# Segment attention in one decoder kernel: output projection as three f32r terms at half height, moved values kept once, and three pieces of work reordered

## The chip, the cores and the metric

The kernel runs on one core of one Trainium2 chip. The metric is the device time of one execution in microseconds (us). The engines are TensorE (PE; its weight loads are listed as PEld), VectorE (DVE), ScalarE (ACT), GpSimd (POOL) and SyncE (SP), which here issues every DMA. Each engine works through its own instructions in program order and waits on semaphores that the others raise.

## The reference

Three layers follow one another, each added to its input and layer-normalised: segment attention, cross attention, and a block with full softmax attention. Only the first is touched:

```
x: 4 x 1024 x 256; 16 heads of 64; segments of 128 tokens
q, k, v = x Wq, x Wk, x Wv          per segment reshaped to (head, 128 positions, 64)
gate = sigmoid(betas)
for each segment of a sequence, with mem and z carried along:
    sq   = elu(q) + 1
    mem += sq^T v ;  z += sum(elu(k) + 1)
    dot  = softmax(q k^T / 8) v
    att  = gate * (sq mem / (rowsum(sq) * z)) + (1 - gate) * dot
    out  = att (128 x 1024) @ Wo (1024 x 256)
x = layernorm(x + out)
```

## The kernel before

`emit_segment_attention` makes 16 iterations of 256 tokens, that is of two segments t = 0, 1. One iteration's work is cut into four units u (two per segment, half of the head groups each). Every engine's program is written out by hand as the same two functions called in turn: `preparation(it)` and `attention(it)`. So the order is fixed in the source, and what differs from one version to another is which semaphore comes late.

`attention(it)` (PE from L373) finishes the attention of iteration it and projects the next one, n = it + 1: K (`project_k`), V (`project_v`), Q (`project_q`), each as a sum of three f32r products hi*hi, hi*lo, lo*hi through `split_matmuls` (L38), with turns of the softmax probabilities (`turn_probs`) and the two products of a unit (`attend`: NUM from the memory, PV from the values) in between. At its end PE turns the input of iteration it + 2 (`turn_x`, into X_BANK), which ACT rounds (`high_x`, L446) and DVE subtracts (`low_x`, L637).

`preparation(it)` (PE from L409) computes scores for the four units (`scores`, L284), turns phi(q) (`turn_phi`, L300), forms the memory products (`memory`, L314) and turns the scaled phi (`turn_phin`, L325). The output projection of the iteration before (`project_out`, L368) is laid between these in three pieces of 8, 4 and 4 chunks. DVE at the same time takes the row maxima (`maxima`, L691), makes phi (`make_phi`, L656), copies turned phi (`take_phi`, L700), adds the memory (`add_memory`, L720) and the residual (`residual`, L743). ACT computes the exponentials (`exp_phi`, `exp_scores`), POOL relu(q) and the scaling of probabilities and phi.

The output projection is plain f32: `att` holds gate and keep parts combined (`combine`, L731, on DVE), its rows split over the two halves e of the 128 partitions, so each chunk is two matmuls of 64 rows, one in each half of the array, into two banks (Y_BANK).

Values travel through memory: ACT copies a unit's V out of X_BANK into `v_stage` (`stage_v`, L455), SP stores it (`values_out`, L185), and after all stores have landed loads it in another layout, 32 small DMAs, into `v_pos` (`values_in`, L193). `v_pos` has two copies, by the parity of the iteration, and `v_stage` has room for all four units. SP's order in an iteration is: store of the normalised rows, residual load, input load, the value stores, the value loads. Banks and rings shared between steps are guarded by waits such as the one of `turn_phin` on `y_added` (L318 to L323: the bank is Y_BANK), or of `project_v` on `v_staged` (X_BANK has one unit at a time).

## Time and profile before

| | us |
|---|---|
| median of 3 runs | 1963.51 (1960.6 to 1967.28) |
| the profiled execution's own time | 1964.41 |
| its span, first to last instruction | 1962.6 |
| busy over the span: PE, DVE, ACT, POOL | 1811.5, 1472.6, 1525.0, 548.0 |
| one iteration of segment attention (key projection to key projection, 295.05 to 344.29) | 49.24 |

The span is what the profiler's records cover; the execution's own time is 1.8 us longer. Segment attention takes about 820 us of the span, the other layers the rest. Below, "the frame" means one iteration in the middle, with its trace times: `attention` from 295.05 to 325.88 on PE, `preparation` from 325.88 to 344.29. A record's duration includes a latency of its own, so neighbours on an engine overlap: what one more instruction costs is the distance from start to start, and what a waiter sees is the end.

### The profile page before, as it was taken

Reading aid. Unit: us, or ns where it says so; the run is one execution under the profiler, and the core shown is the slowest. Engines: PE = TensorE matmul, PEld = TensorE weight load, DVE = VectorE, ACT = ScalarE, POOL = GpSimd, SP = SyncE. Lnnn points to the kernel's source line nnn. Section 1 sums busy time; section 2 is a strip of 40 time slices with the busy share of each in tenths; the row PEclk is TensorE's granted clock in tenths of the full one; section 3 lists DMA queues with packets and bytes.
Section 4 is the critical chain, followed back from the end, with each engine's and each line's share of the span. In section 5 each row is a group of like instructions: output and inputs, shape, how many; then the busy total and the mean of one; then the engine's idle time right before and its main releaser. Section 6 shows DMA issues by size and latency. Waiting matters only on the chain. (4 is left out here: it accounts for less than half of the span.)

```text
span 1962.6 us, 45176 instructions
## 1 busy us (share of the span) xinstructions
PE 1811.5 (92%) x16278; PEld 1231.5 (63%) x16378; DVE 1472.6 (75%) x2829; ACT 1525.0 (78%) x4376; POOL 548.0 (28%) x658
## 2 busy tenths in 40 slices
PE   6999999999999999599999989899999899899996
PEld 5888888888888888469999978422222222222264
DVE  7677777777777777246666656799999999999845
ACT  6777777777777777248888856799999999999853
POOL 2343333333333334205676520000000000000023
PEclk9999999999999999899999989899999999999998
DMA  7223333233322332251101009335325334423001
GB/s 172 44 61 60 60 60 61 61 60 60 61 61 60 61 61 55 64 136 32 43 15 43 15 17 224 130 52 77 46 44 74 58 44 58 74 44 44 1 22 64
DMA packets 139653, 121.73 MB, mean 62 GB/s; under 512 B 78747, under 2 KB 111407, under 8 KB 139439
## 3 DMA queue, kind: packets, MB, share of 16 engines
q1 hardware_dynamic: 139439, 118.88, 30.7%
q8 instruction: 134, 2.20, 0.5%
q14 instruction: 80, 0.66, 0.1%
HBM read 77.29 MB, written 41.53 MB: 61 GB/s over the span
## 5 line engine op out<-in xcount | busy, mean ns | idle before, releaser
L1889 DVE TENSOR_REDUCE s_neg_max<-s_ring 128x1 f32<-128x1024 f32 x512 | 588.7, 1215 | 22.7 <-PE s_ring L1804 22.6
L1852 ACT ACTIVATE s_prob<-s_ring,s_neg_max 128x1024 f32<-128x1024 f32 x512 | 570.6, 1115 | 16.6 <-DVE s_neg_max L1889 16.2
L1817 PE MATMUL s_acc<-s_prob,s_v_norm 128*32 128x256 f32 x4096 | 327.7, 393 | 11.6 <-ACT f_zT_all L1844 10.4
L1804 PE MATMUL s_ring<-f_stack 128*128 128x512 bf16 x924 | 292.2, 390 | 33.2 <-issue 14.3
L492 ACT ACTIVATE a_prob<-a_psum,a_neg_max 128x128 f32<-128x128 f32 x512 | 179.8, 377 | 60.6 <-DVE a_neg_max L691 60.6
L1817 PEld LDWEIGHTS s_acc<-s_prob,s_v_norm 128*32 128x32 f32 x4096 | 81.5, 108 | 229.7 <-issue 215.0
L1804 PEld LDWEIGHTS s_ring<-f_stack 128*128 128x128 bf16 x1024 | 58.7, 97 | 244.4 <-ACT s_prob L1852 225.0
L1872 POOL TENSOR_TENSOR s_v_norm<-f_v_all,s_row_inv 128x64 f32<-128x64 f32 x128 | 37.4, 292 | 570.3 <-DVE s_row_inv L1882 570.3
L586 POOL TENSOR_SCALAR a_relu_ring<-a_qT 128x512 f32<-128x512 f32 x64 | 98.6, 1557 | 343.0 <-ACT a_qT L463 315.7
L731 DVE SCALAR_TENSOR_TENSOR a_att<-a_psum,a_keep_cols,a_num_s 128x128 f32<-128x128 f32 x256 | 72.1, 345 | 134.2 <-ACT a_num_s L514 127.5
L1271 ACT ACTIVATE x_prob<-x_psum,x_neg_max 128x77 f32<-128x77 f32 x512 | 160.8, 337 | 14.2 <-DVE x_neg_max L1428 14.1
L38 PE MATMUL a_psum<-a_xT_hi,a_w_hi 128*128 128x256 f32 x512 | 152.9, 299 | 5.8 <-DVE a_w_lo L629 5.8
L38 PE MATMUL a_psum<-a_xT_lo,a_w_hi 128*128 128x256 f32 x512 | 145.2, 284 | 0.0
L38 PE MATMUL a_psum<-a_xT_hi,a_w_lo 128*128 128x256 f32 x512 | 145.2, 284 | 0.0
L602 POOL TENSOR_TENSOR a_prob<-a_prob,a_row_inv 128x512 f32<-128x512 f32 x128 | 137.4, 1099 | 1.6 <-DVE a_row_inv L696 1.6
L1354 POOL TENSOR_TENSOR x_prob<-x_prob,x_row_inv 128x308 f32<-128x308 f32 x128 | 91.7, 717 | 134.0 <-DVE x_row_inv L1434 134.0
L368 PE MATMUL a_psum<-a_w_out,a_att 64*128 64x256 f32 x1024 | 119.9, 379 | 3.9 <-DVE a_att L731 3.8
L647 DVE TENSOR_SCALAR a_kT<-a_psum 64x256 f32<-64x256 f32 x256 | 107.9, 421 | 12.1 <-PE a_psum L38 6.7
L504 ACT COPY a_probT<-a_psum 128x512 f32<-128x512 f32 x128 | 75.5, 590 | 51.4 <-PE a_psum L337 50.7
L492 ACT ACTIVATION_READ_ACCUMULATOR a_prob<-a_psum,a_neg_max 128x1 f32 x512 | 110.6, 216 | 0.0
L1271 ACT ACTIVATION_READ_ACCUMULATOR x_prob<-x_psum,x_neg_max 128x1 f32 x512 | 110.4, 216 | 0.0
L463 ACT COPY a_qT<-a_psum 64x256 f32<-64x256 f32 x256 | 94.0, 367 | 18.1 <-PE a_psum L38 15.5
(199 smaller groups left out, 4101.2 us busy)
## 6 DMA issues: line engine op xcount, KB each, us to landing
f_stack<-qk_thirds SPq DMA_DIRECT2D x256, 128.0 KB, 6.0
segment_values<-a_v_stage SPq DMA_DIRECT2D x64, 256.0 KB, 3.6
a_v_pos<-segment_values SPq DMA_DIRECT2D x512, 32.0 KB
qk_thirds<-p_third SPq DMA_DIRECT2D x16, 768.0 KB, 7.8
a_x_in<-in_x_dram SPq DMA_DIRECT2D x16, 256.0 KB, 3.2
a_x_res<-in_x_dram SPq DMA_DIRECT2D x32, 128.0 KB, 2.8
after_attention<-a_normed SPq DMA_DIRECT2D x32, 128.0 KB, 2.4
x_x_in<-after_attention SPq DMA_DIRECT2D x32, 128.0 KB, 2.1
```

Of the source, the lines that this page charges most:

```text
L38: last = pe.matmul(out, a, b, start=n == 0, stop=n == len(terms) - 1)
L368: last = pe.matmul(Y_BANK[e][:, 0:D], att[rows(e), c, :, :].rearrange("p m i -> p (m i)"), w_out[rows(e), c, :], start=c == 0, stop=c == H ...
L463: last = act.copy(shift_target(qT, r, e, f), shift_source(bank[f], r, e))
L492: last = act.activation(prob[:, u, n, :], bank[2 * (u % 2) + e][:, gi * P:(gi + 1) * P], ACT.Exp, bias=neg_max[:, u, n:n + 1], accum_out=r ...
L586: pool.tensor_scalar(relu_ring[:, u % 2, :], qT[:, m:m + 4, :, :].rearrange("p a b c -> p (a b c)"), 0.0, None, ALU.max).then_inc(q_relu, 1)
L602: pool.tensor_tensor(part, part, row_inv[:, u, 4 * half:4 * half + 4].unsqueeze(2).to_broadcast([P, 4, P]), ALU.mult).then_inc(prob_ready, 1)
L647: last = dve.tensor_scalar(shift_target(kT, r, e, f), shift_source(bank[f], r, e), 1.0 / KEY_DIV, None, ALU.add)
L1271: last = act.activation(prob[:, t % 2, at:at + CTX], S_BANK[g][:, j * CTX:(j + 1) * CTX], ACT.Exp, bias=neg_max[:, t % 2, g, j:j + 1], acc ...
L1804: last = pe.matmul(ring[n % 3][:, f * HALF:(f + 1) * HALF], k_stack[:, slot, j, kt * P:(kt + 1) * P], q_stack[:, slot, j, f * HALF:(f + 1) ...
L1817: last = pe.matmul(acc[32 * j:32 * j + 32, s], v_norm[:, step // KT % 2, step % 4, j, :], prob[:, step % 4, j, s], start=step % (2 * KT) = ...
L1852: act.activation(prob[:, step % 4, j, :], ring[n % 3][:, :], ACT.Exp, bias=neg_max[:, step % 2, j:j + 1], accum_out=row_sum[:, step % 2, j ...
L1889: dve.tensor_reduce(neg_max[:, step % 2, j:j + 1], ring[n % 3][:, :], AX_X, ALU.max, negate=True).then_inc(max_ready, 1)
```

## The change

Four things are changed, all in segment attention.

1. The output projection is a sum of three f32r products. Wo is loaded to a staging place and split into `w_out_hi` and `w_out_lo` once (ACT and POOL, at the start). `combine` now writes its result in place in `num_s`; a new ACT step `high_att` rounds it to `att_hi`, and a new DVE step `low_att` subtracts to give `att_lo`. `project_out` issues per chunk three terms of two half-height matmuls (96 an iteration instead of 32).
2. `v_pos` has one copy, so `values_in` waits for `pv_done` of the iteration before. `v_stage` holds two units instead of four: `stage_v` of units 2 and 3 waits until the stores of units 0 and 1 of the same iteration have landed. The stores are issued per unit, 8 of half the size instead of 4.
3. The input turn moves behind the last `attend` on PE; `high_x` and `low_x` move from `attention` into `preparation`.
4. The scores of unit 3 move on PE from before the last piece of the output projection to between `memory(1)` and `memory(2)`, and on DVE `maxima(it, 3)` moves behind `add_memory` 0 and 1.

On PE, at the end of `preparation` in the middle of the program (a_e_ring is phi before its turn, a_phi_tok phi turned, a_kT and a_qT the operands of the scores). Before:

```order
L284 MATMUL a_psum<-a_kT,a_qT 128x128 [waits a_exp_done]
L284 MATMUL a_psum<-a_kT,a_qT 128x128 x7
L368 MATMUL a_psum<-a_w_out,a_att 128x256 x8
L314 MATMUL a_psum<-a_v_pos,a_phi_tok 64x64 [waits a_v_landed0,a_phi_tok_ready]
L314 MATMUL a_psum<-a_v_pos,a_phi_tok 64x64 x7
L314 MATMUL a_psum<-a_v_pos,a_phi_tok 64x64 [waits a_phi_tok_ready]
L314 MATMUL a_psum<-a_v_pos,a_phi_tok 64x64 x7
L314 MATMUL a_psum<-a_v_pos,a_phi_tok 64x64 [waits a_mem_added,a_v_landed1,a_phi_tok_ready]
L314 MATMUL a_psum<-a_v_pos,a_phi_tok 64x64 x7
L314 MATMUL a_psum<-a_v_pos,a_phi_tok 64x64 [waits a_mem_added,a_phi_tok_ready]
L314 MATMUL a_psum<-a_v_pos,a_phi_tok 64x64 x7
L325 MATMUL a_psum<-a_ident,a_phin 128x128 [waits a_y_added,a_phin_ready]
```

After (L316 was L300, L300 was L284, L386 was L368, L330 was L314, L341 was L325):

```order
L386 MATMUL a_psum<-a_w_out_hi,a_att_lo 128x256 x2
L330 MATMUL a_psum<-a_v_pos,a_phi_tok 64x64 [waits a_v_landed0,a_phi_tok_ready]
L330 MATMUL a_psum<-a_v_pos,a_phi_tok 64x64 x7
L330 MATMUL a_psum<-a_v_pos,a_phi_tok 64x64 [waits a_phi_tok_ready]
L330 MATMUL a_psum<-a_v_pos,a_phi_tok 64x64 x7
L300 MATMUL a_psum<-a_kT,a_qT 128x128 [waits a_exp_done]
L300 MATMUL a_psum<-a_kT,a_qT 128x128 x7
L330 MATMUL a_psum<-a_v_pos,a_phi_tok 64x64 [waits a_mem_added,a_v_landed1,a_phi_tok_ready]
L330 MATMUL a_psum<-a_v_pos,a_phi_tok 64x64 x7
L330 MATMUL a_psum<-a_v_pos,a_phi_tok 64x64 [waits a_mem_added,a_phi_tok_ready]
L330 MATMUL a_psum<-a_v_pos,a_phi_tok 64x64 x7
L341 MATMUL a_psum<-a_ident,a_phin 128x128 [waits a_y_added,a_phin_ready]
```

The scores of unit 3 now stand behind two memory products; the wait of the turn of phin on `a_y_added` is unchanged.

On DVE, from the end of `attention` to the second `maxima` (a_xT_lo is the input's low part, a_neg_max the row maxima). Before:

```order
L684 TENSOR_TENSOR a_z_gate<-a_z_inv,a_gate_cols 128x16 [waits a_z_step]
L637 TENSOR_TENSOR a_xT_lo<-a_psum,a_xT_hi 128x2x2x64 [waits a_xT_hi_ready]
L637 TENSOR_TENSOR a_xT_lo<-a_psum,a_xT_hi 128x2x2x64
L731 SCALAR_TENSOR_TENSOR a_att<-a_psum,a_keep_cols,a_num_s 128x16x8 [waits a_num_scaled,a_pv_done]
L731 SCALAR_TENSOR_TENSOR a_att<-a_psum,a_keep_cols,a_num_s 128x16x8 x3
L691 TENSOR_REDUCE a_neg_max<-a_psum 128x8 [waits a_scores_done]
L656 SCALAR_TENSOR_TENSOR a_e_ring<-a_e_ring,a_relu_ring 128x512 [waits a_q_relu,a_phi_exp] x2
L691 TENSOR_REDUCE a_neg_max<-a_psum 128x8 [waits a_scores_done]
L696 RECIPROCAL a_row_inv<-a_row_sum 128x8 [waits a_exp_done]
```

After (L788 is `low_att`, L780 `combine`, L740 `maxima`, L686 `low_x`):

```order
L788 TENSOR_TENSOR a_att_lo<-a_num_s,a_att_hi 128x4x16x8 [waits a_att_high]
L780 SCALAR_TENSOR_TENSOR a_num_s<-a_psum,a_keep_cols,a_num_s 128x128 [waits a_num_scaled,a_pv_done]
L780 SCALAR_TENSOR_TENSOR a_num_s<-a_psum,a_keep_cols,a_num_s 128x128 x3
L788 TENSOR_TENSOR a_att_lo<-a_num_s,a_att_hi 128x4x16x8 [waits a_att_high]
L740 TENSOR_REDUCE a_neg_max<-a_psum 128x8 [waits a_scores_done]
L686 TENSOR_TENSOR a_xT_lo<-a_psum,a_xT_hi 128x2x2x64 [waits a_xT_hi_ready]
L686 TENSOR_TENSOR a_xT_lo<-a_psum,a_xT_hi 128x2x2x64
L705 SCALAR_TENSOR_TENSOR a_e_ring<-a_e_ring,a_relu_ring 128x512 [waits a_q_relu,a_phi_exp] x2
L740 TENSOR_REDUCE a_neg_max<-a_psum 128x8 [waits a_scores_done]
L745 RECIPROCAL a_row_inv<-a_row_sum 128x8 [waits a_exp_done]
```

`low_x` has moved from ahead of the last `combine` to behind the first `maxima`, and one of the four `low_att` stands ahead of that `maxima`, with a wait on ACT.

On SP, one iteration up to the first value loads. Before:

```order
L179 DMA after_attention<-a_normed 64x2x256 [waits a_normed_ready]
L179 DMA after_attention<-a_normed 64x2x256
L174 DMA a_x_res<-in_x_dram 64x2x256 [waits a_y_added]
L174 DMA a_x_res<-in_x_dram 64x2x256
L164 DMA a_x_in<-in_x_dram 128x2x256 [waits a_x_turned]
L185 DMA segment_values<-a_v_stage 64x1024 [waits a_v_staged]
L185 DMA segment_values<-a_v_stage 64x1024
L185 DMA segment_values<-a_v_stage 64x1024 [waits a_v_staged]
L185 DMA segment_values<-a_v_stage 64x1024
L193 DMA a_v_pos<-segment_values 8x16x64 [waits a_v_stored1,a_v_stored0]
```

After:

```order
L178 DMA a_x_res<-in_x_dram 64x2x256 [waits a_y_added]
L178 DMA a_x_res<-in_x_dram 64x2x256
L168 DMA a_x_in<-in_x_dram 128x2x256 [waits a_x_turned]
L190 DMA segment_values<-a_v_stage 64x512 [waits a_v_staged]
L190 DMA segment_values<-a_v_stage 64x512
L190 DMA segment_values<-a_v_stage 64x512 [waits a_v_staged]
L190 DMA segment_values<-a_v_stage 64x512
L190 DMA segment_values<-a_v_stage 64x512 [waits a_v_staged]
L190 DMA segment_values<-a_v_stage 64x512
L190 DMA segment_values<-a_v_stage 64x512 [waits a_v_staged]
L190 DMA segment_values<-a_v_stage 64x512
L201 DMA a_v_pos<-segment_values 8x16x64 [waits a_pv_done,a_v_stored1,a_v_stored0]
```

The four stores of two waits are eight stores of four waits; what stands ahead of them is the same.

The diff, cut to its core:

```diff
-        v_stage = sb("v_stage", [P, 2, INNER])
-        v_pos = sb("v_pos", [P, 2, 2, H, DH])
+        v_stage = sb("v_stage", [P, 2, HALF])
+        v_pos = sb("v_pos", [P, 2, H, DH])
...
-        stage = [probs[:, 0:2048], probs[:, 2048:4096], att[:, :, :, :].rearrange("p a b c -> p (a b c)")]
+        stage = [probs[:, 0:2048], probs[:, 2048:4096], v_pos[:, :, :, :].rearrange("p a b c -> p (a b c)")]
+        out_stage = [phi_tok[:, :, :].rearrange("p a b -> p (a b)"), probs[:, 0:2048]]
...
-            def values_out(it, e):
-                sp.wait_ge(v_staged, 4 * it + 2 * e + 2)
+            def values_out(it, u):
+                e, half = u // 2, u % 2
+                sp.wait_ge(v_staged, 4 * it + u + 1)
                 for t in range(2):
                     at = it * TOK + t * P + e * DH
-                    sp.dma_start(v_rows[at:at + DH, :], v_stage[rows(t), e, :]).then_inc(v_stored[e], 16)
+                    sp.dma_start(v_rows[at:at + DH, half * HALF:(half + 1) * HALF], v_stage[rows(t), u % 2, :]
+                                 ).then_inc(v_stored[u % 2], 16)
 
             def values_in(it, t):
                 if t == 0:
-                    for e in range(2):
-                        sp.wait_ge(v_stored[e], 32 * (it + 1))
+                    for n in range(2):
+                        sp.wait_ge(v_stored[n], 64 * (it + 1))
+                if it > 0:
+                    sp.wait_ge(pv_done, 4 * (it - 1) + 2 * t + 2)
                 at = it * TOK + t * P
                 for c in range(H):
-                    sp.dma_start(v_pos[c * 8:(c + 1) * 8, it % 2, t, :, :],
+                    sp.dma_start(v_pos[c * 8:(c + 1) * 8, t, :, :],
                                  v_rows[at:at + P, c * DH:(c + 1) * DH].rearrange("(h i) d -> i h d", i=8)
                                  ).then_inc(v_landed[t], 16)
+
+            def load_out(n):
+                if n == 1:
+                    sp.wait_ge(w_low, 1)
+                for e in range(2):
+                    sp.dma_start(out_stage[n][rows(e), :].rearrange("p (c n) -> p c n", n=D),
+                                 wo.rearrange("(c v) n -> v c n", v=DH)[:, n * 8:(n + 1) * 8, :]
+                                 ).then_inc(wo_landed[n], 16)
...
@@ -362,11 +378,14 @@
                 if chunks[0] == 0:
                     pe.wait_ge(att_ready, 4 * it + 4)
                     if it == 0:
-                        pe.wait_ge(wo_landed, 32)
+                        pe.wait_ge(wo_low, 2)
+                terms = ((att_hi, w_out_hi), (att_hi, w_out_lo), (att_lo, w_out_hi))
                 for c in chunks:
-                    for e in range(2):
-                        last = pe.matmul(Y_BANK[e][:, 0:D], att[rows(e), c, :, :].rearrange("p m i -> p (m i)"), w_out[rows(e), c, :],
-                                         start=c == 0, stop=c == H - 1, skip_group_check=True)
+                    for n, (left, right) in enumerate(terms):
+                        for e in range(2):
+                            last = pe.matmul(Y_BANK[e][:, 0:D], left[rows(e), c, :, :].rearrange("p m i -> p (m i)"),
+                                             right[rows(e), c, :], start=c == 0 and n == 0,
+                                             stop=c == H - 1 and n == 2, skip_group_check=True)
...
+                    if old:
+                        attend(it, u)
                     if u == 3 and it + 2 < ITER:
                         turn_x(it + 2)
-                    if old:
...
-                scores(it, 3)
                 if it > 0:
                     project_out(it - 1, range(12, H))
-                for u in range(UNITS):
-                    memory(it, u)
+                memory(it, 0)
+                memory(it, 1)
+                scores(it, 3)
+                memory(it, 2)
+                memory(it, 3)
...
             def stage_v(it, u):
-                e, half = u // 2, u % 2
                 act.wait_ge(v_done, 4 * it + u + 1)
-                if it > 0:
-                    act.wait_ge(v_stored[e], 32 * it)
-                act.copy(v_stage[:, e, half * HALF:(half + 1) * HALF], X_BANK[:, :]).then_inc(v_staged, 1)
+                if it > 0 or u >= 2:
+                    act.wait_ge(v_stored[u % 2], 64 * it + 32 * (u // 2))
+                act.copy(v_stage[:, u % 2, :], X_BANK[:, :]).then_inc(v_staged, 1)
+
+            def high_out(n):
+                act.wait_ge(wo_landed[n], 32)
+                act.copy(w_out_hi[:, 8 * n:8 * n + 8, :].rearrange("p c n -> p (c n)"), out_stage[n]
+                         ).then_inc(wo_high, 1)
+
+            def high_att(it, u):
+                m = (u // 2) * GR + (u % 2) * 4
+                act.wait_ge(combined, 4 * it + u + 1)
+                if u == 0 and it > 0:
+                    act.wait_ge(y_done, it)
+                act.copy(att_hi[:, :, m:m + 4, :].rearrange("p c m i -> p m c i"),
+                         num_s[:, u % 2, :, :].rearrange("p m (c i) -> p m c i", i=8)).then_inc(att_high, 1)
...
@@ -487,6 +520,8 @@
                 act.wait_ge(max_ready, 4 * it + u + 1)
                 if it > 0:
                     act.wait_ge(prob_turned, 8 * (it - 1) + 2 * u + 2)
+                elif u == 0:
+                    act.wait_ge(wo_low, 2)
...
+                if not old:
+                    high_out(0)
...
+                        if u > 0:
+                            high_att(it, u - 1)
...
-                    if u == 3 and it + 2 < ITER:
-                        high_x(it + 2)
+                    if not old and u == 1:
+                        high_out(1)
...
+                if it > 0:
+                    high_att(it - 1, 3)
...
+                if it + 1 < ITER:
+                    high_x(it + 1)
...
+            for n in range(2):
+                pool.wait_ge(wo_high, n + 1)
+                pool.tensor_tensor(w_out_lo[:, 8 * n:8 * n + 8, :].rearrange("p c n -> p (c n)"), out_stage[n],
+                                   w_out_hi[:, 8 * n:8 * n + 8, :].rearrange("p c n -> p (c n)").bitcast(F32),
+                                   ALU.subtract).then_inc(wo_low, 1)
...
                 dve.wait_ge(phi_turned, 4 * it + u + 1)
+                if it == 0 and u == 0:
+                    dve.wait_ge(wo_low, 1)
...
             def combine(it, u):
-                t, half = u // 2, u % 2
+                half = u % 2
                 dve.wait_ge(pv_done, 4 * it + u + 1)
                 dve.wait_ge(num_scaled, 4 * it + u + 1)
-                if u == 0 and it > 0:
-                    dve.wait_ge(y_done, it)
                 for gi in range(4):
                     g = half * 4 + gi
                     last = dve.scalar_tensor_tensor(
-                        out=att[:, :, t * GR + g, :],
-                        in0=PV_BANK[:, gi * P:(gi + 1) * P].rearrange("p (c i) -> p c i", i=8),
-                        scalar=keep_cols[:, g:g + 1],
-                        in1=num_s[:, u % 2, gi, :].rearrange("p (c i) -> p c i", i=8),
-                        op0=ALU.mult, op1=ALU.add)
-                last.then_inc(att_ready, 1)
+                        out=num_s[:, u % 2, gi, :], in0=PV_BANK[:, gi * P:(gi + 1) * P], scalar=keep_cols[:, g:g + 1],
+                        in1=num_s[:, u % 2, gi, :], op0=ALU.mult, op1=ALU.add)
+                last.then_inc(combined, 1)
+
+            def low_att(it, u):
+                m = (u // 2) * GR + (u % 2) * 4
+                dve.wait_ge(att_high, 4 * it + u + 1)
+                dve.tensor_tensor(att_lo[:, :, m:m + 4, :].rearrange("p c m i -> p m c i"),
+                                  num_s[:, u % 2, :, :].rearrange("p m (c i) -> p m c i", i=8),
+                                  att_hi[:, :, m:m + 4, :].rearrange("p c m i -> p m c i").bitcast(F32), ALU.subtract
+                                  ).then_inc(att_ready, 1)
...
-                    if u == 3 and it + 2 < ITER:
-                        low_x(it + 2)
+                    if old and u > 0:
+                        low_att(it, u - 1)
...
             def preparation(it):
+                if it > 0:
+                    low_att(it - 1, 3)
                 maxima(it, 0)
+                if it + 1 < ITER:
+                    low_x(it + 1)
                 make_phi(it, 0, True)
...
-                maxima(it, 3)
                 add_memory(it, 0)
                 add_memory(it, 1)
+                maxima(it, 3)
```

## Rows read from the trace of the kernel before

**Rows 1.** Windows of two stretches, attention then preparation (stretch, engines' busy us, clock, DMA)

```profile
295.05:325.88 30.83, 30.83 (x295) 27.31 (x294) 19.50 (x55) 21.76 (x55) 7.43 (x8) 1.00 0.30 73
325.88:344.29 18.41, 16.71 (x218) 14.22 (x217) 16.48 (x31) 14.09 (x70) 12.02 (x11) 1.00 0.42 39
```

**Rows 2.** Timeline of TensorE, preparation (start us, duration us, engine, line, work; idle before)

```profile
325.88 2.06 PE L284 MATMUL a_psum<-a_kT,a_qT 64*128 64x128 f32 x32
328.11 3.72 PE L368 MATMUL a_psum<-a_w_out,a_att 64*128 64x256 f32 x32 [0.17 <-DVE a_att L731]
...
332.79 1.16 PE L284 MATMUL a_psum<-a_kT,a_qT 64*128 64x128 f32 x16
...
336.93 0.63 PE L300 MATMUL a_psum<-a_ident,a_e_ring 128*128 128x128 f32 x4 [0.66 <-DVE a_phi_tok L700]
...
342.36 1.15 PE L314 MATMUL a_psum<-a_v_pos,a_phi_tok 128*64 128x64 f32 x32 [0.87 <-DVE a_mem L720]
343.44 1.09 PE L325 MATMUL a_psum<-a_ident,a_phin 128*128 128x128 f32 x8
```

**Rows 3.** Timeline of VectorE, preparation

```profile
325.80 0.76 DVE L637 TENSOR_TENSOR a_xT_lo<-a_psum,a_xT_hi 128x256 fp32r<-128x256 f32 x2 [2.90 <-ACT a_xT_hi L446]
326.93 1.13 DVE L731 SCALAR_TENSOR_TENSOR a_att<-a_psum,a_keep_cols,a_num_s 128x128 f32<-128x128 f32 x4 [0.37 <-ACT a_num_s L514]
327.97 1.22 DVE L691 TENSOR_REDUCE a_neg_max<-a_psum 128x8 f32<-128x1024 f32 x1
329.10 1.28 DVE L656 SCALAR_TENSOR_TENSOR a_e_ring<-a_e_ring,a_relu_ring 128x512 f32<-128x512 f32 x2
...
333.18 1.55 DVE L656 SCALAR_TENSOR_TENSOR a_e_ring<-a_e_ring,a_relu_ring 128x512 f32<-128x512 f32 x1 [0.82 <-POOL a_relu_ring L586]
...
336.70 1.21 DVE L691 TENSOR_REDUCE a_neg_max<-a_psum 128x8 f32<-128x1024 f32 x1
...
339.51 1.24 DVE L700 COPY a_phi_tok<-a_psum 128x512 f32<-128x512 f32 x2
...
342.46 0.75 DVE L743 TENSOR_TENSOR a_y<-a_psum,a_x_res 128x256 f32<-128x256 f32 x2
```

**Rows 4.** Timeline of ScalarE, attention and preparation

```profile
312.69 0.59 ACT L455 COPY a_v_stage<-a_psum 128x512 f32<-128x512 f32 x1
...
319.23 0.60 ACT L504 COPY a_probT<-a_psum 128x512 f32<-128x512 f32 x1
...
326.67 1.18 ACT L481 ACTIVATE a_e_ring<-a_qT 128x512 f32<-128x512 f32 x2
329.22 0.37 ACT L492 ACTIVATE a_prob<-a_psum,a_neg_max 128x128 f32<-128x128 f32 x1 [1.37 <-DVE a_neg_max L691]
```

**Rows 5.** Timeline of TensorE, two neighbours of the f32r key projection

```profile
305.33 0.28 PE L38 MATMUL a_psum<-a_xT_lo,a_w_hi 128*128 128x256 f32 x1
305.45 0.28 PE L38 MATMUL a_psum<-a_xT_hi,a_w_lo 128*128 128x256 f32 x1
```

**Rows 6.** Timeline of SyncE's queue

```profile
310.49 7.36 SPq L185 DMA_DIRECT2D segment_values<-a_v_stage  x4
320.50 12.11 SPq L193 DMA_DIRECT2D a_v_pos<-segment_values  x32
```

**Rows 7.** The value stores' line, issued 310.5 and 311.7

```profile
DMA to landing us min/median/max: 3.3/3.5/3.7
```

**Rows 8.** The page, DMA issues (out, in, count, KB each, us from issue to landing)

```profile
after_attention<-a_normed SPq DMA_DIRECT2D x32, 128.0 KB, 2.4
```

**Rows 9.** Timeline of ScalarE at the program's start

```profile
8.86 1.91 ACT L441 ACTIVATE a_w_hi<-a_att 128x2048 fp32r<-128x2048 f32 x1 [0.64 <-DMA a_att<-in_L_attn_Wv_dram]
...
23.54 1.34 ACT L483 ACTIVATE a_e_ring<-a_kT,a_key_bias 128x512 f32<-128x512 f32 x2 [2.12 <-DVE a_kT L647]
```

**Rows 10.** The output weights' load line

```profile
L208 SPq DMA_DIRECT2D a_w_out<-in_L_attn_Wo_dram x2: 675/1775/2875, 7.8 to 8.5; - x2
...
DMA to landing us min/median/max: 11.1/13.3/15.6
```

More of the change, by code:

```diff
@@ L216, in _ @@
                 if it + 1 < ITER:
-                    for e in range(2):
-                        values_out(it + 1, e)
+                    for u in range(UNITS):
+                        values_out(it + 1, u)
                     for t in range(2):
@@ L353, in attend @@
                 if u > 0:
-                    pe.wait_ge(att_ready, 4 * it + u)
+                    pe.wait_ge(combined, 4 * it + u)
                 for gi in range(4):
                     for e in range(2):
-                        last = pe.matmul(PV_BANK[rows(e), gi * P:(gi + 1) * P], v_pos[:, it % 2, t, e * GR + half * 4 + gi, :],
+                        last = pe.matmul(PV_BANK[rows(e), gi * P:(gi + 1) * P], v_pos[:, t, e * GR + half * 4 + gi, :],
                                          probT[:, e, gi, :], start=True, stop=True)
@@ L570, in _ @@
                 attention(it)
+            high_att(ITER - 1, 3)
         @block.gpsimd
@@ L835, in _ @@
                 attention(it)
+            low_att(ITER - 1, 3)
             residual(ITER - 1)
```

20 lines of the change are left out of this document (11 added, 9 removed).

## The prediction, made before the changed kernel was run

> **What bounds the kernel now.** I read four views in this order: busy time by stretch, TensorE's timeline through `preparation`, then VectorE's, ScalarE's and SyncE's over the same iteration. The first splits one iteration of 49.24 us in two [rows 1]: in the 30.83 us of `attention` PE is busy all the time, in the 18.41 us of `preparation` it is busy 16.71, and DVE 16.48. The clock granted is 1.00 in both, its upper level (2.4 GHz). So `attention` is bound by PE, while in `preparation` two engines are nearly full at once. PE's timeline shows what it waits for there, DVE each time: 0.17 us for the last combine, 0.66 for turned phi, 0.87 for the memory addition [rows 2]. What is taken from PE in `preparation` is a gain only if DVE's chain gets no longer.
>
> All times below are on the frame of this iteration.
>
> **The output projection on PE: less.** The first 32 records (16 matmuls: 8 chunks, each a pair of halves) take 3.72 us, 0.46 a pair; 16 pairs an iteration are 7.4 us [rows 2]. An f32r matmul of 256 columns starts 0.12 us after its neighbour at full height [rows 5]. No f32r matmul at half height is in the trace. Plain f32 at half height is: the scores issue 32 loads of 128 columns and 32 matmul records in 2.06 us [rows 2], 0.064 us a record, 0.129 for two. So a pair lies between 0.12 (both halves at once) and 0.24 us (one after the other, twice rows 5). I take 0.125, near both rows: 48 pairs are 6.0 us, PE has 1.4 us less to do.
> The Trainium skill (TensorE: Matmul & The Clock Gate, section on LDWEIGHTS) gives a load's time as columns / 1.2 in ns, 107 ns for 128 columns, and two loads a pair would make 213 ns and 10.2 us an iteration, more than before. The scores' row disagrees (0.064 us for a load and its matmul record), and the row decides.
>
> **The way from the last combine to the projection: longer.** Before: `combine` 326.93 to 328.06, PE goes on at 328.11 [rows 2, 3]. Now ACT and DVE stand between. `high_att` is 128x512 out of SBUF: the two `exp_phi` of that shape take 1.18 us, the second starting about 0.53 after the first [rows 4], so 0.65 for one and 0.53 of ACT's time. `low_att` is two SBUF inputs of 128x512: two `make_phi` take 1.28 us, 0.60 from start to start and 0.68 for one [rows 3]. With 0.05 to 0.1 a handover (328.06 to 328.11): 328.06, 328.8, 329.5, and `project_out` starts at 329.6. Scores 0 and 1, which covered all but 0.17 of the wait, end at 328.1 (the input turn now stands ahead of them, as before). PE idles 1.5 us.
>
> **DVE's and ACT's chain through `preparation`.** I lay it out step by step, spacings from rows 3 and 4.
> - `maxima(0)` stood at 327.97; behind `low_att` it starts at 329.45. ACT has done `high_att`, two `exp_phi` and `high_x` by 330.3, so `exp_scores(0)`, before at 329.22, starts at 330.7 with the maxima and ends at 333.6 (8 steps, 2.9).
> - `low_x` follows, 0.66 (its pair lasts 0.76), then `make_phi` 0 and 1 (1.2), `maxima(1)` (1.13): 333.6. The idle DVE had here, 0.82 [rows 3] and some more, is used up by this.
> - `scores(2)` waits for `exp_scores(0)`: 333.7 against 332.79. PE's projection (24 pairs, 3.0, to 332.6) and turns end before that, so its 0.7 saved is given back in the wait.
> - `exp_phi(2)` ends at 334.15, `make_phi(2)` runs beside POOL as before (1.55), then a copy, `make_phi(3)`, a copy (0.6 to 0.85 each): `maxima(2)` at 337.8 against 336.70, 1.1 late. The third and fourth `take_phi` stand at 340.6, end at 341.85.
> - The reordered end. `memory(1)` needs the fourth `take_phi`: 341.9 to 342.5. `scores(3)`, before ahead of this, runs from 342.5 and lands at 343.7 (1.16 us for 16 records). `maxima(3)` 343.8 to 345.0, `residual` to 345.7. The turn of phin waits for `y_added`, as the order of PE shows: it starts at 345.7, where before it stood at 343.44 [rows 2, 3]. The 0.87 us wait at the memory products is gone, a wait of 1.2 us at the turn takes its place.
> So `preparation` gets 2.25 us longer. By parts: 1.45 at its head, 0.66 for `low_x`, less 1.0 of idle used, 1.1 at its end. Bounds: if the two roundings cost twice the rows 3.6; if they cost half and `make_phi` meets no POOL work, 1.2.
>
> **The value stores.** Before, `stage_v(2)` copied at 312.69 [rows 4] into space of its own. Now it needs unit 0's store landed. SP comes to this store at 310.49, behind the normalised rows, residual and input [rows 6], whatever `stage_v` does. Its two DMAs were issued at 310.5 and 311.7 and landed 3.3 to 3.7 us later, at up to 315.0, with 256 KB each [rows 7]; they now have 128 KB. I take 314.2; bounds are 313.5 (issued at 311.1 and landed in 2.4, as the normalised rows' 128 KB do [rows 8]) and 315.0. `stage_v(2)` then starts at 314.3, 1.6 late. Behind it in ACT's queue stand the shift of Q, a copy of turned probabilities, now `high_att(1)` (0.53), `stage_v(3)`, `scale_num(2)`, two `exp_phi`, and the copy before at 319.23 [rows 4], for which PE's next turn of probabilities waits. ACT waited for PE some 1.3 us in this stretch; 1.6 + 0.53 - 1.3 is 0.8, by which the copy comes late, and PE's turn with it. With the bounds 0.2 and 1.6. The other `high_att` fall in ACT's idle time, the other `low_att` in DVE's (busy 19.50 of 30.83 [rows 1]).
> That `v_pos` has one copy costs nothing: its 32 loads go from 320.50 to 332.6 [rows 6], the second 16 from 326.6, when the last PV is past (325.9), and `memory(0)` comes at 341. If SP waited for it, 9 us of cover would go first.
>
> **Start and end.** The output weights land 11.1 and 15.6 us after their issue at 7.8 and 8.5 [rows 10], at 18.9 and 24.1; the same bytes come now. ACT rounds each half, 1.91 us, the second from 24.1 to 26.0 in front of `exp_phi` for K, which stood at 23.54 [rows 9]: 2.5 us late. With `low_x` in the first `preparation` 3 us; bounds 0 and 6. At the end the longer way (1.45) meets a projection that is 1.4 shorter: nothing.
>
> **The sum.** 0.8 + 2.25 = 3.05 us an iteration, 15 times: 45.8; with 3 at the start 48.8. On the profiled execution's 1964.4 this is 2013.2; the median of the runs shown is 0.9 lower, so 2012 us.
>
> **Rivals.**
> - *Half-height f32r pairs do not overlap* (0.24 us). The first 24 pairs then end at 335.3, scores 2 at 337.2 instead of 334.7, and every later step of `preparation` follows some 2.5 us late; 15 times 2.5, plus 5.5 at the last projection: 2012 + 43 = 2055. For it: no such row. Against: at half height 32 loads and 32 matmuls of 128 columns take only 2.06 us [rows 2]. 12 in 100.
> - *The stores land early and the roundings are cheap*: 0.2 + 1.2 = 1.4 an iteration, 21 and 3: 1964.4 + 24 - 0.9 = 1988. For it: the 2.4 us of [rows 8]. 15 in 100, with what lies between.
> - *The vector engines take it in*, faster: PE's 1.4 us less and the 0.87 wait filled by scores 3, with the combine-to-projection way covered: 2.3 x 15 = 34, 1930. The place is `residual`: it decides from the point where DVE ends it before PE ends the memory products, at 343.4. DVE has 1.93 us idle in `preparation` [rows 1] and gets 1.26 of work and 1.5 of waiting more, so I don't believe it. 6 in 100.
> - *No change*: store early, half the additions hidden, 0 an iteration within 0.4. 5 in 100.
>
> **The numbers.** The forecast has 62 in 100, its own range 1998 to 2032. From 1982 to 2046 it holds that, most of the second rival and the space up to the first. About 0.3% is what a measurement of this kernel can tell from no change: faster 0.07, within it 0.05, slower 0.88.
>
> **What would show it.** The f32r projection records 0.06 us apart (0.12: first rival). A new PE wait of about 1.5 us before `project_out`, one of about 1.2 before the turn of phin put down to the residual, and none before the second memory products. An ACT wait of some 1.6 us at `stage_v(2)` for the store. An iteration of 52.3 us with PE busy below 46.5. It is wrong if PE reaches the turn of phin later than `y_added`.

## The result and the profile after

The changed kernel takes 2010.49 us (median of 4 runs, 2006.14 to 2011.54) against 1963.92 (4 runs, 1960.6 to 1967.28): ratio 1.0233, 95% interval 1.021 to 1.0256. It is slower by 46.6 us; forecast were 2012 us and slower.

Its page (busy us and share of the span) and, below it, windows over one quiet iteration in the middle, cut at TensorE's start of the projection (the columns of [rows 1]):

```profile
span 2009.1 us, 46517 instructions
...
PE 1825.9 (91%) x16890; PEld 1236.7 (62%) x16890; DVE 1517.8 (76%) x2893; ACT 1555.4 (77%) x4442; POOL 557.1 (28%) x660
```

```profile
299.99:332.36 32.37, 29.52 (x366) 26.42 (x367) 26.72 (x61) 21.56 (x89) 16.51 (x15) 1.00 0.19 27
332.36:351.49 19.13, 17.54 (x178) 15.15 (x176) 11.81 (x29) 15.93 (x40) 2.94 (x2) 1.00 0.51 106
sum 51.50, PE 47.05 PEld 41.57 DVE 38.53 ACT 37.49 POOL 19.45; mean PE 23.53 PEld 20.79 DVE 19.27 ACT 18.74 POOL 9.73
```

An iteration is 51.50 us, of which PE is busy 47.05; before it was 49.24 with 47.54 ([rows 1], both added). So PE has 0.5 us less to do and is idle 4.45 us instead of 1.70. (PE's sum over the program, 1825.9 against 1811.5 before, says nothing of this: the trace of the kernel before lacks 100 of the 1024 records of one matmul line of a later layer. From the first to the last turn of phin, PE is busy 704.5 us, before 712.3.) TensorE's timeline, which answers to [rows 2]:

```profile
296.75 2.06 PE L300 MATMUL a_psum<-a_kT,a_qT 64*128 64x128 f32 x32
299.99 0.39 PE L386 MATMUL a_psum<-a_w_out_hi,a_att_hi 64*128 64x256 f32 x2 [1.18 <-DVE a_att_lo L788]
300.21 0.28 PE L386 MATMUL a_psum<-a_w_out_lo,a_att_hi 64*128 64x256 f32 x2
300.33 0.28 PE L386 MATMUL a_psum<-a_w_out_hi,a_att_lo 64*128 64x256 f32 x2
...
303.01 1.09 PE L316 MATMUL a_psum<-a_ident,a_e_ring 128*128 128x128 f32 x8
304.06 1.16 PE L300 MATMUL a_psum<-a_kT,a_qT 64*128 64x128 f32 x16
...
308.03 0.63 PE L316 MATMUL a_psum<-a_ident,a_e_ring 128*128 128x128 f32 x4 [0.81 <-DVE a_phi_tok L751]
...
311.31 1.28 PE L330 MATMUL a_psum<-a_v_pos,a_phi_tok 128*64 128x64 f32 x32 [1.05 <-DVE a_phi_tok L751]
312.52 1.16 PE L300 MATMUL a_psum<-a_kT,a_qT 64*128 64x128 f32 x16
313.62 1.15 PE L330 MATMUL a_psum<-a_v_pos,a_phi_tok 128*64 128x64 f32 x32
315.77 0.96 PE L341 MATMUL a_psum<-a_ident,a_phin 128*128 128x128 f32 x7 [1.00 <-DVE a_y L797]
```

Rows of two matmuls start 0.12 us apart: the two halves of a pair together take what one matmul at full height takes. The first 8 chunks take 3.02 us to the start of what follows (299.99 to 303.01), before 3.65; all 16 take 6.2, before 7.3. The waits were 0.17, 0.66 and 0.87; now they are 1.18 for the low part of att, 0.81 and 1.05 for turned phi, 1.00 for the residual. From the first scores to the turn of phin (296.75 to 315.77) `preparation` takes 19.02 us; before 17.56 (325.88 to 343.44). VectorE over the same stretch, beside [rows 3]:

```profile
297.43 1.12 DVE L780 SCALAR_TENSOR_TENSOR a_num_s<-a_psum,a_keep_cols,a_num_s 128x128 f32<-128x128 f32 x4 [3.20 <-ACT a_num_s L549]
299.24 0.69 DVE L788 TENSOR_TENSOR a_att_lo<-a_num_s,a_att_hi 128x512 fp32r<-128x512 f32 x1 [0.68 <-ACT a_att_hi L487]
299.85 1.22 DVE L740 TENSOR_REDUCE a_neg_max<-a_psum 128x8 f32<-128x1024 f32 x1
...
304.55 0.84 DVE L705 SCALAR_TENSOR_TENSOR a_e_ring<-a_e_ring,a_relu_ring 128x512 f32<-128x512 f32 x1 [0.32 <-ACT a_e_ring L514]
...
307.81 1.21 DVE L740 TENSOR_REDUCE a_neg_max<-a_psum 128x8 f32<-128x1024 f32 x1
...
313.73 1.23 DVE L740 TENSOR_REDUCE a_neg_max<-a_psum 128x8 f32<-128x1024 f32 x1 [0.67 <-PE a_psum L300]
314.88 0.75 DVE L797 TENSOR_TENSOR a_y<-a_psum,a_x_res 128x256 f32<-128x256 f32 x2
```

The combine starts 0.68 us behind the first scores, before 1.05: the one step that comes earlier. Everything behind `low_att` comes later, and the residual ends at 315.63, 0.14 ahead of the turn that waits for it. ScalarE (beside [rows 4]), then SyncE's queue and the landing of the stores (beside [rows 6, 7]):

```profile
298.59 0.62 ACT L487 CAST a_att_hi<-a_num_s 128x512 fp32r<-128x512 f32 x1 [1.27 <-DVE a_num_s L780]
...
335.71 0.58 ACT L475 COPY a_v_stage<-a_psum 128x512 f32<-128x512 f32 x1 [1.63 <-DMA segment_values<-a_v_stage]
```

```profile
332.02 8.40 SPq L190 DMA_DIRECT2D segment_values<-a_v_stage  x8
...
DMA to landing us min/median/max: 2.4/2.8/3.1
```

The `stage_v` of unit 2 waits 1.63 us for the store of unit 0. `preparation` is 19.02 in nearly every iteration, but the whole iteration varies between 50.97 and 52.79 us with the landing of the stores (the last, 50.34, aside; mean 51.63 over 15, before 49.14).

Over the program: the first turn of phin comes at 57.00 instead of 48.88 (+8.1), the last at 831.38 instead of 785.99 (+45.4), so 37.3 come from 15 iterations; 1.1 more falls behind, to the 46.5 us of the span. That 1.1 is no finding: over all the runs below, what follows the last turn of phin takes between 1172.7 and 1179.8 us. At the start, GpSimd's subtraction that makes `w_out_lo`, and VectorE beside it:

```profile
20.49 4.61 POOL L656 TENSOR_TENSOR a_w_out_lo<-a_phi_tok,a_w_out_hi 128x2048 fp32r<-128x2048 f32 x1 [18.90 <-ACT a_w_out_hi L479]
25.26 4.58 POOL L656 TENSOR_TENSOR a_w_out_lo<-a_prob,a_w_out_hi 128x2048 fp32r<-128x2048 f32 x1 [0.16 <-ACT a_w_out_hi L479]
```

```profile
25.83 4.55 DVE L710 SCALAR_TENSOR_TENSOR a_e_ring<-a_e_ring,a_kT 128x512 f32<-128x512 f32 x1 [2.33 <-ACT a_e_ring L516]
...
31.02 0.68 DVE L710 SCALAR_TENSOR_TENSOR a_e_ring<-a_e_ring,a_kT 128x512 f32<-128x512 f32 x1
```

VectorE's instruction of 0.68 us took 4.55 and ended (30.38) 0.5 us after GpSimd's (29.84).

### The profile page after: what moved, and what is told of

It is laid out like the page before. It is cut to its first block and busy times, and to the rows that moved or that the text cites. A ratio compares the mean times of both kernels' runs of the same rounds, so it can differ in the third digit from the quotient of the medians.

```text
span 2009.1 us, 46517 instructions
## 1 busy us (share of the span) xinstructions
PE 1825.9 (91%) x16890; PEld 1236.7 (62%) x16890; DVE 1517.8 (76%) x2893; ACT 1555.4 (77%) x4442; POOL 557.1 (28%) x660
## 5 line engine op out<-in xcount | busy, mean ns | idle before, releaser
L1863 PE MATMUL s_ring<-f_stack 128*128 128x512 bf16 x1024 | 315.3, 391 | 14.5 <-ACT s_prob L1911 8.1
L780 DVE SCALAR_TENSOR_TENSOR a_num_s<-a_psum,a_keep_cols,a_num_s 128x128 f32<-128x128 f32 x256 | 72.1, 344 | 121.0 <-ACT a_num_s L549 120.5
L527 ACT ACTIVATION_READ_ACCUMULATOR a_prob<-a_psum,a_neg_max 128x1 f32 x512 | 116.1, 227 | 0.0
L1487 DVE TENSOR_REDUCE x_neg_max<-x_psum 128x4 f32<-128x308 f32 x128 | 60.8, 475 | 56.0 <-PE x_psum L38 52.4
L38 PEld LDWEIGHTS a_psum<-a_xT_hi,a_w_hi 128*128 128x128 f32 x512 | 98.6, 193 | 7.0 <-issue 6.3
```

Of the source, the lines that this page charges most:

```text
L38: last = pe.matmul(out, a, b, start=n == 0, stop=n == len(terms) - 1)
L527: last = act.activation(prob[:, u, n, :], bank[2 * (u % 2) + e][:, gi * P:(gi + 1) * P], ACT.Exp, bias=neg_max[:, u, n:n + 1], accum_out=r ...
L1863: last = pe.matmul(ring[n % 3][:, f * HALF:(f + 1) * HALF], k_stack[:, slot, j, kt * P:(kt + 1) * P], q_stack[:, slot, j, f * HALF:(f + 1) ...
```

## The experiments

"Iteration" is from turn of phin to turn of phin in the profiled run, "preparation" from the first scores to the turn of phin. Ratios are to the kernel before, run beside each.

**Stores (part 2).** `v_stage` gets four places again, its stores stay per unit:

```diff
-        v_stage = sb("v_stage", [P, 2, HALF])
+        v_stage = sb("v_stage", [P, UNITS, HALF])
...
-                if it > 0 or u >= 2:
-                    act.wait_ge(v_stored[u % 2], 64 * it + 32 * (u // 2))
+                if it > 0:
+                    act.wait_ge(v_stored[u % 2], 64 * it)
```

> The changed kernel with v_stage given room for four units again (the stores stay per unit and half-size, v_pos stays single). Theory (the vector engines' chain plus the store wait set the iteration): ScalarE's wait for the store at stage_v(2), 1.6 us in the frame looked at and more in some iterations, is gone, every iteration takes the same time, about 51.0 us instead of 51.3 to 52.8, and the total falls by 0.45 to 1.0 us x 15, 7 to 15 us, to 1996 to 2004. Rival (the wait lies in slack, the loss is all in preparation): no change, 2010 within 4.

Measured: 2000.44 us, ratio 1.0172 (1.0147 to 1.0196), iterations of 50.95 us throughout, `preparation` unchanged. (The last takes 50.36, the mean is 50.91.) So the wait costs 51.63 - 50.91 = 0.7 us an iteration in the mean, 10 us in all, and it is what makes iterations differ.

**Input turn (part 3) undone.** `turn_x` ahead of the last `attend`, `high_x` and `low_x` back in `attention`:

```diff
-                    if old:
-                        attend(it, u)
                     if u == 3 and it + 2 < ITER:
                         turn_x(it + 2)
+                    if old:
+                        attend(it, u)
```

> The changed kernel with part 3 undone alone: input turn ahead of the last attend, high_x and low_x back in attention. Theory: low_x leaves the chain of preparation (0.66 less), but high_x again stands before scale_num(3) and puts off the last combine by 0.5: 0.15 us an iteration less, 2 us in all, 2008. Rival (the moved turn costs its 0.66 in full): 10 us less, 2000. Other rival (the move is what pays for part of the rest): 8 us more, 2018.

Measured: 2016.47 us, ratio 1.0256 (1.0233 to 1.0279), 6 us more than the changed kernel: against my theory, and near the second rival's 2018. TensorE at the start of the projection (timeline), where the changed kernel waits 1.18:

```profile
197.57 0.39 PE L386 MATMUL a_psum<-a_w_out_hi,a_att_hi 64*128 64x256 f32 x2 [1.88 <-DVE a_att_lo L788]
...
199.17 0.42 PE L386 MATMUL a_psum<-a_w_out_hi,a_att_hi 64*128 64x256 f32 x2
```

Most of the 6 us does not come from the order of the steps. `preparation` takes about 19.13 us in nine of the 15 iterations with a projection, 0.11 more than in the changed kernel, 18.98 in the last, and 20.5 in the other five. These five differ in TensorE's clock. Windows over the first 8 chunks of one of the five and of its neighbour (columns of [rows 1]):

```profile
197.57:201.86 4.29, 4.29 (x48) 4.07 (x48) 3.62 (x5) 3.18 (x17) 2.46 (x2) 0.66 0.75 73
250.26:253.29 3.03, 3.03 (x48) 2.90 (x49) 3.03 (x4) 2.19 (x12) 1.19 (x1) 1.00 0.72 83
```

The granted clock is 0.66 instead of 1.00 in the mean: part way through it falls to its lower level (1.2 GHz), and the pairs then stand 0.21 us apart instead of 0.12. ScalarE's next `exp_phi` waits 1.26 us for the turns of phi that stand behind. Five times 1.4 us is 7, of the 7.4 by which the 15 iterations of the profiled run are longer than those of the changed kernel. The granted clock over the program is lower in all four runs (0.970 to 0.974 against 0.975 to 0.978). All 15 iterations have a wait of 1.73 to 1.90 there; why the clock falls in five of them is not shown.

On the path the move is nearly even beside the split. With it `combine` starts 0.70 us earlier behind the first scores (0.68 instead of 1.38) and `make_phi(2)` 0.71 earlier (7.80 behind them instead of 8.51). But from `make_phi(2)` to `maxima(2)` it is 3.26 us instead of 2.67, as `make_phi` 2 and 3 now run beside GpSimd (0.84 and 1.36 us). With the move undone they take 0.69 and 0.93. VectorE's timeline there:

```profile
254.83 0.69 DVE L705 SCALAR_TENSOR_TENSOR a_e_ring<-a_e_ring,a_relu_ring 128x512 f32<-128x512 f32 x1 [0.32 <-ACT a_e_ring L514]
...
257.50 1.21 DVE L740 TENSOR_REDUCE a_neg_max<-a_psum 128x8 f32<-128x1024 f32 x1
```

**Last scores and memory additions (part 4) undone:**

```diff
-                memory(it, 0)
-                memory(it, 1)
-                scores(it, 3)
-                memory(it, 2)
-                memory(it, 3)
+                for u in range(UNITS):
+                    memory(it, u)
...
-                add_memory(it, 0)
-                add_memory(it, 1)
                 maxima(it, 3)
+                add_memory(it, 0)
+                add_memory(it, 1)
```

(with `scores(it, 3)` behind `turn_phi(it, 3)`).

> The changed kernel with part 4 undone alone: scores of unit 3 and maxima(3) where they stood. Theory: the residual no longer waits behind the scores and maxima of unit 3, the turn of phin starts 1.3 us earlier: 15 x 1.3 = 20 us less, 1990; the wait for the memory addition (0.9 before) is back but lies under it. Rival (the reorder fills TensorE's wait and is a gain): 0.87 us an iteration more, 13 us, 2023.

Measured: 1989.94 us, ratio 1.012 (1.0095 to 1.0145), `preparation` 17.80 instead of 19.02, as the theory said. TensorE's waits over one iteration (us in total, times, longest):

```profile
PE a_psum L386 <- DVE a_att_lo L786: 1.2, 1, 1.2
PE a_psum L330 <- DVE a_mem L769: 0.9, 1, 0.9
PE a_psum L316 <- DVE a_phi_tok L749: 0.8, 1, 0.8
PE a_psum L38 <- ACT a_v_stage L473: 0.7, 1, 0.7
PE a_psum L330 <- DVE a_phi_tok L749: 0.2, 1, 0.2
```

The wait of 1.00 for the residual is gone, the 0.9 for the memory addition is back, and that for phi at the memory products falls from 1.05 to 0.2.

**Split projection (part 1) undone**, parts 2 to 4 kept: `project_out` in f32 from `w_out` and `att`, no `high_att`, no `low_att`.

> The changed kernel with part 1 undone alone: plain f32 output projection, one att, no rounding steps, no weight split at the start; parts 2, 3 and 4 stay. Theory: the way from the last combine to project_out falls by 1.4 us and the whole chain of preparation with it, although TensorE's work grows by 1.4: 1.4 x 15 = 21 and 5 to 8 at the start, 1981 to 1985. Rival (TensorE's work is the bound, the f32r terms are the one part that gains): 1.4 x 15 more, less 8 at the start, 2023.

Measured: 1982.02 us, ratio 1.0078 (1.0052 to 1.0103), `preparation` 17.48, the first turn of phin at 52.11. The split costs 28.5 us, 4.9 of them at the start.

**GpSimd's subtraction in pieces:** the 2048 columns of L656 as four instructions of 512.

```diff
-                pool.tensor_tensor(w_out_lo[:, 8 * n:8 * n + 8, :].rearrange("p c n -> p (c n)"), out_stage[n],
+                for part in range(4):
+                    cs = slice(8 * n + 2 * part, 8 * n + 2 * part + 2)
+                    last = pool.tensor_tensor(w_out_lo[:, cs, :]...
```

> The changed kernel with GpSimd's two subtractions for w_out_lo (128x2048) cut into four of 128x512 each. Theory (at the start VectorE's first make_phi, 4.55 us instead of 0.68, stands behind a GpSimd instruction that is under way): it lasts at most about 1.9 us, the first turn of phin in preparation comes near 54 instead of 57.0, iterations stay as they are, 3 us less in all. Rival (VectorE is slowed by the traffic, not held by one instruction): it lasts 4 us and more as before, no change.

Measured: the first turn of phin at 53.61, 3.4 us earlier, iterations as before it; one run, 2003.7 us. The five other runs with the whole instructions and the split have that turn between 56.5 and 58.7 us, the two combined kernels below, with the pieces, at 52.3 and 51.4. VectorE's timeline:

```profile
26.30 0.69 DVE L713 SCALAR_TENSOR_TENSOR a_e_ring<-a_e_ring,a_kT 128x512 f32<-128x512 f32 x1 [1.61 <-ACT a_e_ring L516]
...
30.33 1.29 DVE L713 SCALAR_TENSOR_TENSOR a_e_ring<-a_e_ring,a_kT 128x512 f32<-128x512 f32 x1 [0.94 <-ACT a_e_ring L516]
```

The 4.55 us were GpSimd's instruction: with the pieces none of VectorE's four takes more than 1.29 (1.80 in the combined kernels), while one takes 4.4 to 5.1 in each of the six runs with whole ones.

**Residual first.** In the changed kernel VectorE does `residual` ahead of `add_memory(it, 0)` instead of behind `maxima(it, 3)`.

> The changed kernel with the residual ahead of add_memory(0) on VectorE, all else as it is (scores and maxima of unit 3 stay where part 4 put them). Theory: the wait of the turn of phin for the residual (1.0 us) goes and no other takes its place, preparation from 19.0 to 17.9 us, 16 us less in all, 1994. Rival (the reordered scores themselves are what costs, the residual is only the last of several that are late): less than 5 us.

Measured: 1994.9 us, ratio 1.0157 (1.0132 to 1.0181), `preparation` 17.95; no wait of TensorE for the residual is left. So part 4 loses mostly by what it puts in front of the residual on VectorE: about 15 us come back, of the 20 to 22 that undoing the whole part gives.

**A shorter way to the projection.** In the changed kernel ScalarE does `high_att(3)` behind its two `exp_phi`, VectorE `low_att(3)` behind `maxima(0)`, and TensorE the two products with att_hi of all chunks of a piece ahead of those with att_lo.

> The changed kernel with a shorter way to the projection and nothing else: ScalarE does the last rounded half of att behind its two exponents of the turned phi, VectorE its rest behind the first maxima, and TensorE does the two high terms of all pieces' halves ahead of the low one of each. Theory (the way att, high part, rest ends last there and is 1.2 us of wait): part of that wait goes, between 0.75 us an iteration (what TensorE shows) and 1.4 (what the chain has in front of it), so 1989 to 1999 us. Rival (what is gained there is given back at the next wait, for phi): no change, 2007 to 2013.

Measured: 1995.7 us, ratio 1.016 (1.0138 to 1.0181), `preparation` 18.24 (-0.78); the wait of 1.18 became one of 0.46 for att_hi. The theory holds, at its lower end in the iteration. The waits behind it, for phi and for the residual, are as long as they were.

**Part 3 alone on the kernel before:**

> The kernel before with part 3 alone: input turn behind the last attend, high_x and low_x in preparation. Theory: the last combine comes 0.5 us earlier, but the projection still waits for the scores ahead of it, and later steps for TensorE: 49.2 us an iteration as before, within 4 us of it. Rival (the move is worth what it is in the changed kernel, where undoing it cost 6): 6 us faster.

Measured: 1949.79 us (6 runs), ratio 0.9927 (0.9908 to 0.9947): 14 us faster, beyond both answers. Iterations of 48.07 us. VectorE's timeline (first scores here at 325.76, in [rows 2] at 325.88):

```profile
326.11 1.13 DVE L731 SCALAR_TENSOR_TENSOR a_att<-a_psum,a_keep_cols,a_num_s 128x128 f32<-128x128 f32 x4 [3.48 <-ACT a_num_s L514]
327.16 1.21 DVE L691 TENSOR_REDUCE a_neg_max<-a_psum 128x8 f32<-128x1024 f32 x1
328.29 0.74 DVE L637 TENSOR_TENSOR a_xT_lo<-a_psum,a_xT_hi 128x256 fp32r<-128x256 f32 x2
...
332.62 0.69 DVE L656 SCALAR_TENSOR_TENSOR a_e_ring<-a_e_ring,a_relu_ring 128x512 f32<-128x512 f32 x1 [1.07 <-ACT a_e_ring L481]
...
335.28 1.21 DVE L691 TENSOR_REDUCE a_neg_max<-a_psum 128x8 f32<-128x1024 f32 x1
```

The combine starts 0.35 us behind the scores instead of 1.05, and `low_x` fills an idle stretch: 1.07 us of idle are left even so. `make_phi(2)` comes 6.86 behind the scores instead of 7.30, and in 0.69 instead of 1.55 ([rows 3]). The reason is GpSimd's scaling of probabilities. Its rows, of the kernel before and of this one:

```profile
333.15 2.48 POOL L602 TENSOR_TENSOR a_prob<-a_prob,a_row_inv 128x512 f32<-128x512 f32 x2
```

```profile
333.00 2.66 POOL L602 TENSOR_TENSOR a_prob<-a_prob,a_row_inv 128x512 f32<-128x512 f32 x2
```

Before, GpSimd began at 333.15, 0.03 us ahead of VectorE (333.18), which was held; now VectorE is first by 0.38 us. From `make_phi(2)` to `maxima(2)` it is 2.66 us instead of 3.52. Two of TensorE's three waits (0.66 and 0.17) are gone. That these 0.86 us come from the order of the two engines is shown by one iteration of the kernel before itself, the third. There VectorE starts as far behind the first scores as in its neighbours (7.29 us), but GpSimd comes 0.03 us behind it and not ahead. The rows of VectorE and of GpSimd:

```profile
137.09 0.69 DVE L656 SCALAR_TENSOR_TENSOR a_e_ring<-a_e_ring,a_relu_ring 128x512 f32<-128x512 f32 x1 [0.82 <-ACT a_e_ring L481]
```

```profile
137.12 3.00 POOL L602 TENSOR_TENSOR a_prob<-a_prob,a_row_inv 128x512 f32<-128x512 f32 x2
```

Now it is GpSimd that is held (3.00 instead of 2.48), `maxima(2)` follows 2.66 us behind `make_phi(2)`, and `preparation` takes 16.70 us instead of 17.56, the iteration 48.37 instead of 49.24. The third iteration of the next experiment's kernel does the same (17.90 instead of 18.77). So of the 1.31 us that part 3 takes from `preparation` (17.56 to 16.25), 0.86 are the turned order of the two engines and 0.44 the earlier combine.

**Part 4 alone on the kernel before:**

> The kernel before with part 4 alone (the last scores ahead of the second memory products on TensorE, the last maxima behind the additions to memory on VectorE). Theory (the last scores then wait for the last phi, and the next iteration's phi input begins later): +1.1 us an iteration as in the changed kernel, 1980 us. Rival (it fills TensorE's 0.87 us wait for the memory additions): 0.87 x 15 = 13 less, 1951 us.

Measured: 1984.1 us, ratio 1.0101 (1.008 to 1.0122), `preparation` 18.77 instead of 17.56. TensorE's waits:

```profile
PE a_psum L325 <- DVE a_y L745: 1.0, 1, 1.0
PE a_psum L314 <- DVE a_phi_tok L702: 0.7, 1, 0.7
PE a_psum L300 <- DVE a_phi_tok L702: 0.7, 1, 0.7
```

The wait for the memory addition has become two others, 1.0 and 0.7. The theory's time came roughly (1980), but not by the wait that it named, of the last scores for phi: the longest is that for the residual.

**Part 3 with VectorE's end in the order additions, residual, last maxima, on the kernel before:**

> The kernel before with part 3 (the turn of x behind the last attend) and VectorE's last steps in the order additions 0 and 1, residual, last maxima. Theory: TensorE's 0.87 us wait for the additions goes, the iteration is 48.07 - 0.87 = 47.2 us, and the time 1937 us; the last exponents come 1.35 us later, within the slack that ScalarE shows there. Rival (that slack is not there, and the products behind the last scores wait for them): 1950 us or more.

Measured: 1955.74 us (7 runs), ratio 0.9961 (0.9947 to 0.9975): not better than part 3 alone. The 0.87 us wait did go (`preparation` 15.58 instead of 16.25), but the iteration is 48.25 instead of 48.07. TensorE and GpSimd:

```profile
342.43 0.63 PE L325 MATMUL a_psum<-a_ident,a_phin 128*128 128x128 f32 x4 [0.56 <-POOL a_phin L593]
```

```profile
341.27 2.04 POOL L593 TENSOR_TENSOR a_phin<-a_phi_tok,a_s_inv 128x512 f32<-128x512 f32 x2 [1.80 <-DVE a_s_inv L707]
```

The next turn of phin waits for GpSimd, which waits for VectorE's sums, and these stand behind the same steps as before. The rival's number came nearer, by another mechanism than the one it named.

**Combined**, all of the split kept: four places, old order of part 4, pieces on GpSimd, the shorter way; and the same with that end order:

> The changed kernel with room for four units in v_stage, part 4 undone, GpSimd's subtraction in pieces, and a shorter way to the projection: ScalarE's two exp_phi ahead of high_att(3), VectorE's maxima(0) ahead of low_att(3), TensorE's hi terms of a piece ahead of its lo terms, so that the first 16 pairs wait for high_att alone. Theory: 0.7 (store), 1.2 (order), 0.75 to 1.4 (way) an iteration less than 51.6, about 48.6 us, and 3 at the start: 1958 to 1966, level with the kernel before or under it. Rival (the pieces share one chain, only the largest counts): 1.4 x 15, 1989.

> The combined kernel (all of the projection's split kept; four stages, old order of the last scores, pieces on GpSimd, the shorter way to the projection) with VectorE's last steps in the order additions 0 and 1, residual, last maxima. Theory: its 0.9 us wait for the additions goes, 48.99 - 0.9 = 48.1 us an iteration, 1948 us. Rival (the wait moves on to another operand): 1961 us as without.

Measured: 1961.31 us (12 runs), ratio 0.9992 (0.9979 to 1.0004), iterations of 48.99; and 1966.32 us (12 runs), ratio 1.001 (0.9998 to 1.0021), 49.17 us, again with 0.6 of wait for GpSimd's phin. The first came as forecast; for the second the rival was right (the wait moves on, no gain), not the theory's 1948. The changed kernel's loss can be taken back, the split then costs what part 3 gains. Part 3 alone beats both kernels, and the first combined one by 12 us.

## Why the prediction was right

By parts, from ratios times 1964 us: part 3 -14 (alone), part 4 +20 (alone), part 2 +10 (0.0078 of the three, less these), part 1 +30 (1.0233 less 1.0078): 46. This closes by construction, as part 2 is what the others leave; it was never run alone on the kernel before. Undone one at a time in the changed kernel they come out as +30, +12 (the staging), -5 and +22, which is about 60. So parts 4 and 2 cost about the same by either count, and part 3 is the one that depends on its surroundings: beside the split its gain of 5 us is nearly all TensorE's clock, which falls in five iterations without it.

- *The pair*: taken 0.125 us, measured 0.118; the first rival (0.24) is out. The whole projection is 1.1 us shorter an iteration, not 1.4, as each of its three pieces has some 0.2 us more at its edges. PE busy fell only to 47.05, not below 46.5 as forecast, and PE gains nothing by it: in `preparation` each of its waits is ended by VectorE. The Trainium skill gives 107 ns for a load of 128 columns (TensorE: Matmul & The Clock Gate, section on LDWEIGHTS). As a cost from load to load this does not hold here at full clock: two loads and two matmuls repeat every 118 ns.
- *The way to the projection*: from the start of combine to TensorE 2.67 us forecast, 2.56 measured; the idle is 1.18 instead of 1.5, as combine starts 0.37 earlier behind the scores. The experiment on this way shows that its wait was on the path.
- *`low_x`*: here the step was wrong. I charged 0.66 us, but behind `low_x` VectorE still waits 0.32 us for ScalarE's `exp_phi` before `make_phi(2)`, so nothing of it is on the path. And I wrote only that the input turn stood ahead of the scores as before, and left out that moving it behind the last `attend` lets the last products, and with them combine, come earlier. Part 3 is a gain of 14 us alone and of 5 here, not a cost.
- *`make_phi(2)` to `maxima(2)`*: 3.26 us where I laid out 3.65, as GpSimd's scaling no longer met it from its start (0.84 instead of 1.55), though it met `make_phi(3)` (1.36). With the point above, `preparation` grew by 1.46 and not 2.25.
- *The end*: +1.1 forecast; 1.22 and 1.07 by undoing it in two ways. Right, with its mechanism.
- *The stores*: wait 1.6 forecast, 1.63 in the frame. In the mean the rest of the iteration grew by 51.63 - 19.02 - 31.68 = 0.93, forecast 0.8; 0.7 of it is the wait; in the frame it grew by 0.80. What I took for one fixed landing time is one that varies. That the single `v_pos` costs nothing fits the trace, in which no engine waits for the value loads between 57 and 831 us; no run tries it alone.
- *The start*: 3 forecast, 8.1 measured, outside its bounds (0 to 6). I counted ScalarE's rounding and forgot that GpSimd's subtraction would hold VectorE: 3.4 by the run in pieces, of the 4.9 that go with part 1 (57.00 less 52.11). The other 3.2 stand with parts 2 to 4 and are not taken apart; part 3 alone on the kernel before has that turn at 52.70, 3.8 later, but undoing part 3 in the changed kernel moves it only by 0.5.

The sum: 37.3 + 8.1 + 1.1 = 46.5 measured, 45.8 + 3 + 0 = 48.8 forecast. The forecast owes its closeness in part to luck, errors of opposite sign: 8.5 too much in the iterations and 6.2 too little around them. The direction rests on what held: the split shortens the engine that waits and lengthens the two it waits for.

## What to carry to other kernels

Work taken off an engine is a gain only where that engine ends the wait; first look at who releases it, and count what the split adds to the releaser. When a step is moved, price the place that it leaves as well as the one it goes to, and look which instructions of VectorE and GpSimd will now meet: here 0.03 us of order decided over 0.86 us an iteration. Before a difference of a few us is put down to an order of steps, look whether all iterations share it and at which clock they ran. A removed wait is worth only its distance to the next one: look one step further down the same chain (sums, then GpSimd, then TensorE).
